# A weight's rounding and a bank's copy moved ahead of the turned probabilities at the end of a pair of heads

## The reference, cut to what matters

```python
q2 = (q @ wiq.T + biq).reshape(N, H, D).transpose(1, 0, 2)      # k2, v2 likewise
scores = jnp.einsum('hnd,hmd->hnm', q2, k2) * scale + mask[None]
attn = jax.nn.softmax(scores, axis=-1)
out = jnp.einsum('hnm,hmd->hnd', attn, v2)
...
q = feature_map(x @ Wq + bq)       # mixer; feature_map(x) = exp(-x*x/2)
k = feature_map(x @ Wk + bk)
coeff = jnp.sum(q * k, axis=-1, keepdims=True)                   # per head
mixed = (coeff * (x @ Wv + bv)) @ Wo + bo
```

## Time and profile before

| | |
|---|---|
| median of 3 runs | 470.89 us (469.66 to 470.96) |
| the profiled execution's own time | 471.46 us |
| its span | 469.6 us |
| busy: TensorE, VectorE, ScalarE, GpSimd | 461.2, 337.6, 255.9, 159.7 us |
| mean granted TensorE clock | 1.000 (full) |
| chain that ended last, by engine | TensorE 86%, VectorE 6%, DMA 3%, ScalarE 3% |

### The profile page before, as it was taken

How to read it: one execution, slowest core, us unless ns; L and a number is a source line. 1 busy time by engine, 2 the same in 40 slices (tenths; PEclk the granted TensorE clock), 3 DMA queues, 4 the chain that set the end, 5 groups by cost and what they waited for, 6 DMA issues and landing times.

```text
span 469.6 us, 7280 instructions
## 1 busy us (share of the span) xinstructions
PE 461.2 (98%) x2505; PEld 428.1 (91%) x2505; DVE 337.6 (72%) x774; ACT 255.9 (54%) x420; POOL 159.7 (34%) x186
## 2 busy tenths in 40 slices
PE   7999999999999999999999999999999999999996
PEld 5999999999998888999999998999998888888885
DVE  5969877667635337578888987897885893586394
ACT  5444433333332335778779788887965362153270
POOL 5447667677768741002130211202045000040200
PEclk9999999999999999999999999999999999999999
DMA  8878766665554473676676756867589754210463
GB/s 292 289 243 244 237 192 182 183 160 168 145 169 135 136 254 127 204 242 216 191 240 201 233 188 194 258 209 248 176 237 356 258 209 137 88 45 1 163 242 134
DMA packets 39656, 91.85 MB, mean 196 GB/s; under 512 B 7250, under 2 KB 21298, under 8 KB 39492
## 3 DMA queue, kind: packets, MB, share of 16 engines
q1 hardware_dynamic: 34852, 85.38, 57.0%
q0 software_dynamic: 4256, 5.09, 3.5%
q10 hardware_dynamic: 512, 0.92, 0.5%
HBM read 77.90 MB, written 13.47 MB: 195 GB/s over the span
## 4 chain that ended last, share of the span: by engine, by line
PE 86%; DVE 6%; DMA 3%; ACT 3%; issue 1%; SPq 0%; POOL 0%; DVEq 0%; ACTq 0%
PE PS L1323 31%; PE PS L1333 28%; PE PS L1328 16%; PE PS L1453 3%; PE PS L1383 2%; PE PS L1577 2%; PE PS L1441 2%; DMA turn<-U 1%; DMA U<-turn 1%; DVE w_lo L931 1%; DVE U L1107 1%; PE PS L1310 1%; ACT U L704 1%; PE PS L1581 1%; DVE probT_lo L1072 1%
## 5 line engine op out<-in xcount | busy, mean ns | idle before, releaser
L931 DVE TENSOR_TENSOR w_lo<-raw,w_hi 128x1024 fp32r<-128x1024 f32 x85 | 103.0, 1224 | 45.0 <-ACT w_hi L594 44.9
L594 ACT ACTIVATE w_hi<-raw 128x1024 fp32r<-128x1024 f32 x86 | 90.1, 1055 | 77.0 <-PE PS L1333 45.9
L510 POOL DMA_INDIRECT table<-evalue,where x96 | 101.5, 1057 | 45.8 <-issue 28.2
L1323 PE MATMUL PS<-xT_hi,w_hi 128*128 128x384 f32 x320 | 62.1, 335 | 0.0
L1328 PE MATMUL PS<-xT_hi,w_lo 128*128 128x384 f32 x320 | 61.9, 334 | 0.0
L1323 PE MATMUL PS<-xT_lo,w_hi 128*128 128x384 f32 x320 | 61.9, 334 | 0.0
L1323 PEld LDWEIGHTS PS<-xT_hi,w_hi 128*128 128x128 f32 x320 | 56.0, 188 | 0.4 <-issue 0.4
L1323 PEld LDWEIGHTS PS<-xT_lo,w_hi 128*128 128x128 f32 x320 | 56.0, 188 | 0.0
L1328 PEld LDWEIGHTS PS<-xT_hi,w_lo 128*128 128x128 f32 x320 | 56.0, 188 | 0.0
L1333 PE MATMUL PS<-w_hi,T_hi 128*128 128x512 f32 x144 | 40.0, 391 | 0.0
L1333 PE MATMUL PS<-w_hi,T_lo 128*128 128x512 f32 x144 | 39.9, 389 | 0.0
(11 more groups left out here) (242 smaller groups left out, 803.2 us busy)
## 6 DMA issues: line engine op xcount, KB each, us to landing
raw<-weights SPq DMA_DIRECT2D x84, 512.0 KB, 5.1
turn<-U SPq DMA_DIRECT2D x16, 576.0 KB, 3.7
U<-turn SPq DMA_DIRECT2D x64, 144.0 KB, 3.0
U<-key_dram SPq DMA_DIRECT2D x32, 192.0 KB, 4.1
mask<-weights SPq DMA_DIRECT2D x9, 512.0 KB, 5.4
table<-Q SPq DMA_DIRECT2D x4, 576.0 KB, 9.2
V<-conv SPq DMA_DIRECT2D x4, 512.0 KB, 5.0
U<-table POOLq DMA_DIRECT2D x3, 576.0 KB, 6.6
```

Of the source, the lines that this page charges most:

```text
L510: pool.indirect_dma_start(tables[g], bass.IndirectOffsetOnAxis(ap=where[:, k:k + 1], axis=0), evalue[:, k:k + 1], None, bounds_check=N * N ...
L594: act.activation(w_hi[slot][:], raw[slot][:], ACT.Copy).then_inc(hi_ready[slot], 1)
L931: dve.tensor_tensor(w_lo[slot][:], raw[slot][:], w_hi[slot][:].bitcast(F32), ALU.subtract).then_inc(lo_ready[slot], 1)
L1323: pe.matmul(o, w_hi[slot][:, k * P:(k + 1) * P], src[part][:, k, :], start=(k == 0 and part == 0), stop=False)
```

## The change

At the end of each pair but the last, ScalarE now rounds the weight for the second column job of the next pair (`slot_use(14 + 4 * j)`, which was `ahead[0]` at the head of the next pair), then copies the mixer value bank, and only then rounds the turned probabilities of the first head. At the head of a pair only pair 0 still rounds `ahead[0]`. VectorE's order isn't changed. In `pv`, TensorE waits first for `pT_hi` and runs the three products with the high part, then waits for `pT_ready` and runs the three with the low part; before, it waited for `pT_ready` and took high and low in turn.

```diff
-                split_hi(*ahead[0])
+                if j == 0:
+                    split_hi(*ahead[0])
                 split_hi(*ahead[1])
...
-                turned_hi(j, 0)
-                mix_value(j, rv)
+                if last:
+                    turned_hi(j, 0)
+                    mix_value(j, rv)
+                else:
+                    split_hi(*slot_use(14 + 4 * j))
+                    mix_value(j, rv)
+                    turned_hi(j, 0)
                 if j:
                     out_hi(j - 1)
...
-                pe.wait_ge(pT_ready, j * 2 + (h + 1))
+                pe.wait_ge(pT_hi, j * 2 + (h + 1))
                 pe.wait_ge(vs_ready, j + 1)
                 pe.wait_ge(o_summed, j * 2 + (h + 1))
-                for m in range(NT):
-                    for part in range(2):
+                for part in range(2):
+                    if part:
+                        pe.wait_ge(pT_ready, j * 2 + (h + 1))
+                    for m in range(NT):
                         last = pe.matmul(PS[:, 7, 0:N], vs[:, m, h, :], probT[part][:, m, :],
                                          start=(m == 0 and part == 0), stop=(m == NT - 1 and part == 1))
```

## The result

The changed kernel takes 477.29 us (median of 4 runs, 477.16 to 479.21) against 470.92 for the kernel before (now 4 runs): a ratio of 1.0143, 95% interval 1.0121 to 1.0166. The forecast was 476.3, range 474.3 to 478.6. The profiled execution took 477.33 us with a span of 475.3.

The account below looks back on a forecast made before the run. TensorE, busy 98% of the span, was taken to bound the kernel. Terms 0.78 + 0.82 + 2.5 + 1.95 - 0.56 - 0.21 gave +5.3 us: 476.8 from the profiled execution, 476.2 from the median; forecast 476.3, range 474.3 to 478.6.

Parts of the forecast that it names:

- The wait for R: Ordinary pair's end: ScalarE's copy, then the rounding, wait for R, the end of `rv`'s last matmul; +0.82 us in pair 1.
- The restart inside `pv`: Before the three low products: TensorE pays 0.10 us to restart after its wait; free restarts would save 0.7 us.
- The weight's rounding: Moved to the pair's end, it is worth nothing, because it only lengthens ScalarE's idle in the next pair.
- the idle for a weight: Sign in the next pair: ScalarE's idle for a weight, 2.61 us in pair 2, grows by a microsecond.
- G - R: Pair's end: from `rv`'s last matmul (R) to the start of the job after `pv(j,0)` (G); 2.88 us before in pair 1.
- `rv` no longer starts late: Pairs 1 and 2: late starts of value job `rv`, 0.14 and 0.07 us, go away: -0.21 us.
- the terms of pair 3: Pair 3's end: subtract, four value-tile multiplies of 1.96 us, hop and restart, summed to R + 5.15, +1.95 us.
- (a): Rival: later softmax and turn through memory make probabilities land late in five pairs, 2.5 us more, 479; chance 0.12.
- pair 4's term: Pair 4's end: probabilities landed late, so putting the copy first takes R + 4.26 to R + 3.70: -0.56 us.
- (b): Rival: less is lost, as restarts are free (-0.7) and pair 3's multiplies arrive sooner (-0.5): 474.5 to 475; chance 0.09.
- (c): Rival in `pv`: the three high products cover the rest, so only pair 4 counts, -1.38 us: 469.5; chance 0.04.
- (d): Rival: late landings like pair 4's happen in more pairs without the profiler; four more of seven tie at 471; chance 0.04.

Follow-up runs that it names:

- copy-alone kernel: The changed kernel, but with each weight rounded at the head of its pair: 477.21 us, ratio 1.0135 to the kernel before.
- products-alone kernel: The changed kernel with ScalarE's order as before the change, so only the high products first in `pv` remains: 470.28 us against 470.65, ratio 0.9998.
- weight alone: The changed kernel with the turned probabilities rounded ahead of the bank's copy again, the weight's early rounding and high products first kept: 471.96 us, ratio 1.0025.
- two later traces of the kernel before: The kernel before, unchanged, run twice more for its traces on a slower chip, where the kernel before took 499.46 us.
- pair-4 kernel: The changed kernel with ScalarE's old order and weights at the head, except the copy ahead of the turned probabilities in pair 4: 471.87 us against 470.96.
- order alone: The changed kernel with the six products in their old order, all waiting for the low part: 480.44 us, ratio 1.0205.
- milder-delay kernel: The changed kernel with SyncE reading the first head's blocks back right after the second head's are written: 492.30 us, ratio 1.0446.

## Why the prediction was right, point by point

**The wait for R.** Right, and shown twice: by ScalarE's idle before line 781, and by the copy-alone kernel, which has the whole cost. The sum in an ordinary pair was 0.05 short: R + 3.70 forecast, 3.75 in pairs 1, 2, 5 and 6. The first hop, the copy, the rounding and the subtract were each 0.01 to 0.02 longer.

**The restart inside `pv`.** In the changed kernel's rows three low products take from 225.91 to 226.54, 0.63, against 3 x 0.175 without a stop: the 0.10 was paid, and the three low products of the products-alone kernel, which didn't wait, take 0.52 (286.90 to 287.42). The trace differs here from what I drew from the Trainium skill ("TensorE: Matmul & The Clock Gate", Step-by-step: what each phase is for), that the weights could be in place when the wait ends. TensorE's weight loads in the changed kernel:

```profile
225.91 0.47 PEld L1461 LDWEIGHTS PS<-probT_lo,vs 128*128 128x128 f32 x3 [0.92 <-DVE probT_lo L1078]
```

The first load behind the wait starts at 225.91 with its matmul, while the next job's loads start at 226.37, 0.17 ahead of theirs (226.54). Here the pull-ahead didn't reach over the wait. One reading of mine was off beside it, without weight in the sum: three high products right behind the scores take 0.63 us, not 0.52 (286.27 to 286.90), though TensorE waits for nothing there.

**The weight's rounding.** Worth nothing, as said, as long as the copy is next; about 1.7 us of cost if the probabilities are next (weight alone against products alone). One sign that I had named didn't come: the idle for a weight in the next pair didn't grow by a microsecond. In the changed kernel ScalarE waits for no weight from pair 2 to pair 6. Nor does it at the head of pair 2 in the two later traces of the kernel before, so the 2.61 us of the earlier trace rows, my cover for this step, were one execution's too. That the moved step cost nothing is therefore shown by the copy-alone kernel, and not by that idle.

**Pair by pair.** G - R in the two traces: pair 0 3.09 to 3.88 (0.78 forecast, 0.79 measured); pair 1 +0.87 (0.82); pairs 2, 5, 6 together +2.7 (2.5); pair 3 +1.89 (1.95); pair 4 4.26 to 3.76, -0.50 (-0.56). `rv` no longer starts late: R - G of the pair before falls by 0.20 and 0.18 in pairs 1 and 2 (-0.38, where I had read -0.21), and grows by 0.14 in pair 4, behind the wait for the multiplies. With 0.12 more at the kernel's start that makes 5.6 us at the last G (330.39 to 336.01) and 5.7 in the span. Two slips in my working change nothing: the terms of pair 3 add up to R + 5.13 and not 5.15, and in rival (a) R + 0.49 is G + 18.3 and not 18.5, which leaves 0.5 us to spare and not 0.6.

**The step that was mis-sized** is pair 4's term. For the traced execution the sum was good (5.3 forecast, 5.6 to 5.7 measured); between the medians the change costs 6.4, where 476.3 stood for 5.4. -0.56 holds against that execution's R + 4.26. I then took its 0.57 us above the median off the changed kernel's time as well, as though the changed kernel kept what made this execution slow; its own traced execution (477.33) lies at its median (477.29). Over the five traces the old order has 2.85 to 4.26 there, and 3.75 is a loss of 0.9 against the lowest and a gain of 0.5 against the highest. Against the lowest, the other terms as measured (0.79 + 0.87 + 2.7 + 1.89 + 0.90 - 0.24 + 0.12) give 7.0, against the highest 5.6; the medians differ by 6.4. That the forecast of the median came within 1 us is in part luck, since the two ends are 1.4 us apart. Whether pair 4's landing is what spreads the kernel before's own runs (469.66 to 472.27) wasn't shown, and the pair-4 kernel's trace has other delays of the same size.

**The rivals.** (a) The lag didn't spread: no landing stands in TensorE's waits. (b) Restarts weren't free. (c) The high products first hid 0.52 us a pair (order alone against the changed kernel) and no more. (d) is half right: late landings do vary, in pair 4 and once in pair 5, but no trace of an undelayed kernel has one in four of seven pairs.

**Open.** Why pair 4's read-back delays TensorE by up to 1.4 us in some executions, and pair 5's in another. No version beat the kernel before by more than the measurement can tell.

## What to carry to other kernels

On an engine that executes in order, an instruction that waits for the bottleneck engine's last result makes everything behind it wait too; put the links of a critical chain ahead of it, unless their own input comes later still. To price such a swap, measure everything from the event that it waits for (here R), and add the chain link by link to the next instruction of the bottleneck: that sum was right to 0.05 us in an ordinary pair. A stall seen in one trace is one draw; take a second trace before counting its removal as a gain.

## What the runs showed of the hardware

TensorE's waits of 0.6 to 1.2 us in the changed kernel left its granted clock at 1.00 around them: it is 1.00 from 200 to 340 us. In the milder-delay kernel of the new order TensorE stood 3.13 us at the end of pair 0, and the products after it ran at the lower level, 1.2 GHz: three take 1.33 us instead of 0.79, eight of the next job 2.76 instead of 1.55. TensorE's timeline:

```profile
206.12 1.33 PE L1461 MATMUL PS<-probT_hi,vs 128*128 128x384 f32 x3 [3.13 <-ACT probT_hi L692]
...
208.64 2.76 PE L1329 MATMUL PS<-T_hi,w_hi 128*128 128x384 f32 x8
```

The mean granted clock of that stretch (200 to 215 us) is 0.77, and that of the next 15 us is 1.00.

The same kernel fell to it once more after two stops of 1.64 and 0.60 us at the end of pair 5 (the next job's first eight matmuls take 2.51), and not after stops of 1.60 and 0.60 in pair 2 (1.56). The old order with the same delay did so after stops of 4.41 and 2.73 us in pairs 0 and 2 (eight take 2.76 both times), and in pair 4 part of the way through `pv`, after a stop of 2.57. Part of what late landings cost (23.4 and 21.5 us) is therefore clock and not wait.
